# First attention of a two-layer block: the values' result turned ahead of the scores in two steps, and the last rows normalised a step sooner

## The reference

```
z    = einsum('nshd,ed->nshe', x, fm_w) + fm_b
v, k, q = (concat([exp(z), exp(-z)]) for x in (ctx, ctx, layernorm(x)))
scores  = einsum('nqhd,nkhd->nhqk', q, k) / sqrt(128)     # 16 heads of 16 features
attn    = softmax(scores)
out     = einsum('nhql,nlhd->nqhd', attn, v) @ fc_w.T + fc_b
x = x + out
```

## Time and profile before

| | |
|---|---|
| three runs | 350.15, 351.95 (median), 352.85 us |
| the profiled execution | 349.49 us, of which the span is 347.7 us |
| PE busy in the span | 303.8 us (87%) |
| DVE busy | 210.8 us (61%) |
| ACT busy | 166.4 us (48%) |
| POOL busy | 151.5 us (44%) |
| mean granted clock of TensorE | 0.973 of full speed |

### The profile page before, as it was taken

How to read it: one execution, slowest core, us unless ns; L and a number is a source line. 1 busy time by engine, 2 the same in 40 slices (tenths; PEclk the granted TensorE clock), 3 DMA queues, 4 the chain that set the end, 5 groups by cost and what they waited for, 6 DMA issues and landing times.

```text
span 347.7 us, 6257 instructions
## 1 busy us (share of the span) xinstructions
PE 303.8 (87%) x1956; PEld 208.6 (60%) x1957; DVE 210.8 (61%) x673; ACT 166.4 (48%) x276; POOL 151.5 (44%) x201
## 2 busy tenths in 40 slices
PE   7789799999988989899988977999999999999800
PEld 2344244545445547558865533788888888888700
DVE  5767375481558976857778696455455455455316
ACT  3567667667464545531555153444444444444314
POOL 5964796510102150110124056376666666664310
PEclk9999989999999999999999999999999999999965
DMA  7404130300000150000002100111111111122055
GB/s 210 142 2 160 58 154 1 126 0 6 0 1 2 38 205 1 3 0 2 0 0 74 49 0 27 28 56 47 47 45 46 45 45 45 45 45 38 25 163 214
DMA packets 9784, 19.08 MB, mean 55 GB/s; under 512 B 2337, under 2 KB 3713, under 8 KB 9761
## 3 DMA queue, kind: packets, MB, share of 16 engines
q1 hardware_dynamic: 7264, 13.67, 12.0%
q0 software_dynamic: 2496, 5.12, 5.5%
HBM read 13.99 MB, written 4.65 MB: 54 GB/s over the span
## 4 chain that ended last, share of the span: by engine, by line
PE 66%; DVE 18%; ACT 5%; DMA 4%; issue 3%; POOL 2%; SPq 1%; POOLq 0%; DVEq 0%; ACTq 0%
PE ps L1199 54%; PE ps L1705 5%; DVE xn L543 2%; DVE mx L588 2%; DMA dnT<-y_dram 2%; PE ps L1207 2%; PE ps L1304 2%; DVE stats L531 2%; PE ps L1680 1%; DVE hg L707 1%; ACT r_hot L1152 1%; PE ps L1311 1%; POOL rstd L366 1%; ACT dist L1147 1%; DVE g3r L631 1%
## 5 line engine op out<-in xcount | busy, mean ns | idle before, releaser
L490 POOL DMA_INDIRECT y_dram<-yb,dst_row x39 | 38.4, 986 | 32.2 <-DVE yb L932 31.9
L365 POOL TENSOR_SCALAR rstd<-mv 128x4 f32<-128x4 f32 x16 | 3.8, 236 | 99.7 <-DVE mv L534 99.7
L484 POOL DMA_INDIRECT xg<-xn_dram,src_row x39 | 38.0, 974 | 13.2 <-PE ps L1680 8.5
L1199 PE MATMUL ps<-dnT,hhT 128*128 x312 | 41.4, 275 | 0.6 <-DVE yb L932 0.6
L1167 ACT ACTIVATE gl<-ps 128x512 f32<-128x512 f32 x39 | 23.3, 597 | 38.6 <-PE ps L1199 38.6
L1199 PEld LDWEIGHTS ps<-dnT,hhT 128*128 128x128 f32 x312 | 37.8, 191 | 4.1 <-issue 0.8
L1046 ACT ACTIVATE ex<-ps 77x1024 f32<-77x1024 f32 x32 | 30.9, 1016 | 17.3 <-PE ps L1199 17.3
L588 DVE TENSOR_REDUCE mx<-ps 128x4 f32<-128x308 f32 x64 | 27.7, 472 | 18.9 <-PE ps L1199 18.2
L1173 ACT ACTIVATE hhT<-ps 128x512 f32<-128x512 f32 x39 | 23.3, 598 | 31.3 <-PE ps L1705 31.3
L1199 PE MATMUL ps<-uphi,xghi 128*128 x78 | 33.9, 435 | 1.1 <-DVE xglo L920 0.6
L918 DVE CAST xghi<-ps 128x128 fp32r<-128x128 f32 x39 | 11.4, 291 | 37.1 <-PE ps L1680 37.1
(11 more groups left out here) (229 smaller groups left out, 608.4 us busy)
## 6 DMA issues: line engine op xcount, KB each, us to landing
uplo<-in_up_dram SPq DMA_DIRECT2D x8, 512.0 KB, 4.4
dnT<-in_down_dram SPq DMA_DIRECT2D x8, 256.0 KB, 4.6
dnT<-y_dram SPq DMA_DIRECT2D x4, 512.0 KB, 6.3
xn_dram<-xn SPq DMA_DIRECT2D x4, 256.0 KB, 2.4
out_dram<-x SPq DMA_DIRECT2D x4, 256.0 KB, 2.4
x<-in_x_dram SPq DMA_DIRECT2D x3, 256.0 KB, 3.2
xg<-xn_dram,src_row POOLq DMA_INDIRECT x39, 2.7
y_dram<-yb,dst_row POOLq DMA_INDIRECT x39, 2.3
```

Source lines behind the costliest of these rows:

```text
L484: g.indirect_dma_start(xg[:, k % XR, :], None, xn_dram, bass.IndirectOffsetOnAxis(ap=src_row[:, k:k + 1], axis=0)).then_inc(gathered[k % X ...
L490: g.indirect_dma_start(y_dram, bass.IndirectOffsetOnAxis(ap=dst_row[:, k:k + 1], axis=0), yb[:, k % 2, :], None).then_inc(scattered[k % 2] ...
L1199: return pe.matmul(out_, lhsT, rhs, start=start, stop=stop, skip_group_check=True)
```

## The change

In steps 4 and 8, the first steps of batches 1 and 2, PE issues `turn_values(G - 2)` before `scores(G)` and no longer after it. In step 4 three products that nothing reads go ahead of it into bank 7, behind a wait for `normalise(1)`, which is the last reader of that bank. On DVE, the four instructions that normalise the rows of batch 3 move from the end of step 4 to the end of step 3, ahead of the two first maxima of step 4. Nothing is removed.

```diff
@@ VectorE, loop over G
-                if g == 0 and b + 2 < NB:
-                    layernorm_apply(0, b + 2)
+                if G in (0, NG - 1):
+                    layernorm_apply(0, 2 + G // (NG - 1))
@@ TensorE, loop over G
                 if G in (NG, 2 * NG):
                     for job in maxima(G, 0):
                         max_job(*job)
+                    if G == NG:
+                        pe.wait_ge(dve_on, G - 2)
+                        fill(3)
+                    turn_values(G - 2)
                 if turned:
                     queries(b + 2)
                 elif G < STEPS:
@@
-                if G >= 2:
+                if G >= 2 and G not in (NG, 2 * NG):
                     turn_values(G - 2)
                 if G >= 1:
                     values(G - 1)
```

## The result

The changed kernel took 346.71 us in the median of four runs (346.43 to 347.60), the kernel before 351.94 in four (350.15 to 352.85): ratio 0.986, 95% interval 0.982 to 0.991. Faster, by 5.2 us between these medians where the sum said 2.75. Twelve more runs of the changed kernel, alternating with the kernel before (experiment 7), give 0.990 (0.987 to 0.994), that is 3.4 us. Medians and ratios here leave out slow runs, those over 1.5% above the fastest of their kernel, such as two of twelve in each of experiments 1, 3, 4 and 9. The profiled execution took 346.59 us with a span of 344.8, against 349.49 and 347.7: 2.9 us.

A forecast was written before the change was run, and what follows sets the result against it. PE was taken to bound the kernel (66% of the chain), losing in step 4 to idling, half clock and late DVE. Terms -1.9 - 1.15 + 0.3 = -2.75 us gave a forecast median of 349.2, range 346.8 to 352.7.

The forecast's parts named there:

- the sum: Whole kernel: -1.9 in step 4, -1.15 in step 5, +0.3 in step 8, together -2.75 us.
- PE's queue and ACT: Steps 4 to 6: scores(5) near 45.0, released by ACT's exponentials, 0.2 behind PE's own queue; scores(6) at 49.0.
- The unread products hide: Step 4: three products (0.75) and the turn (0.53) fit the idle stretch at no cost, cutting it from 1.62 to 0.34.
- The moved xn instructions: Step 3 on DVE: POOL holds them from 37.93 to about 41.5, but maxima and normalise(2) stay in time, cost nothing.
- Step 8 costs 0.3: Step 8: the moved turn waits for ACT's copy and PE loses about 0.3, with bounds 0 and 0.85.
- The loss of step 4 is idle, half clock and late DVE in a row: Steps 4 and 5: three successive losses, with 1.9 us to gain in step 4 and 1.15 in step 5.
- the step that POOL's AFFINE_SELECTs don't hold DVE: Step 4 without half clock: xn instructions run unheld beside POOL's AFFINE_SELECTs, from about 45.7, done by 46.8.
- a rival with a chance of 0.20: Step 4: the clock doesn't fall in the timed runs, so the old order loses little; result 0, 352.0 us; chance 0.20.
- held all the same: Step 4: no clock fall, but POOL's AFFINE_SELECTs hold DVE's xn instructions until about 49.4; gain 2.1, 349.9 us; chance 0.07.
- a gain of more than 1%: Whole kernel: a measured time of 348.4 us or less, reached only with a lucky median; chance 0.20.
- its range: Whole kernel, measured time: 346.8 to 352.7 us, from the forecast's lower scatter to the no-clock-fall rival with its median's scatter.

The follow-up runs named there:

- experiment 7: Changed kernel run again with no edit, twelve runs alternating with the kernel before; median 348.22 us, ratio 0.990.
- experiments 1: Kernel before with only the four xn instructions of batch 3 moved to the end of step 3, PE's order as before; median 348.40 us, ratio 0.993.
- experiment 3: Changed kernel with step 8 put back as before, its turn no longer ahead of the scores; median 347.70 us, ratio 0.991.
- experiment 4: Changed kernel without the three unread products and their wait, both turns still ahead; median 349.58 us, ratio 0.995.
- experiment 9: Kernel before with only POOL reordered: b2 conversions first, selG and g3 built after the xn instructions; median 347.88 us, ratio 0.992.
- Experiments 5: Kernel before with only the three unread products and their wait added in step 4's idle stretch; median 352.05 us, ratio 1.001.
- experiment 6: Kernel before run and profiled again with no edit; median 351.17 us, ratio 1.000.
- Experiment 2: Changed kernel with the four xn instructions back at the end of step 4, PE's order kept; median 348.11 us, ratio 0.992.
- experiment 11: Kernel before with only seven more unread products in two later PE stalls; median 350.28 us, ratio 0.999.
- experiment 8: Changed kernel with seven more unread products in two later PE stalls; median 347.11 us, ratio 0.987.

## Why the prediction was right, and where its reasons were not

*PE's queue and ACT.* Right to 0.1: the sum had `scores(4)` to `scores(5)` at 3.2 and `scores(5)` to `scores(6)` at 4.0; measured 3.24 and 3.90, with ACT as the new releaser by 0.18, as said.

*The unread products hide.* Right: they and the turn take 1.09 of the idle 1.62, and 0.53 stay where the sum had 0.34.

*The moved xn instructions.* Right: DVE goes on to the maxima 3.43 us behind their start (38.10 to 41.53), where the sum had 3.5, and no one waits for it. (The fourth of them ends at 42.00, held by a MEMSET of POOL, but the maxima start beside it.)

*Step 8 costs 0.3.* Right: a wait of 0.30, and 0.33 by experiment 3.

*The loss of step 4 is idle, half clock and late DVE in a row.* The order of these was right, their shares were not. The prediction gave 1.9 us to step 4, for the turn in the idle stretch and the clock, and 1.15 to DVE's lateness. What failed is the step that POOL's AFFINE_SELECTs don't hold DVE, read from the earlier trace rows. From it followed that without the half clock the xn instructions would be done by 46.8 and the change be worth nothing, a rival with a chance of 0.20. Experiments 5 and 6 are that case, and in both the xn instructions end past 49.5 (49.54 and 49.62) and `scores(6)` come 12.9 behind `scores(3)`. The true split, at `scores(9)`: 0.63 for the clock of the one profiled execution (31.39 to 30.76) and 2.18 for the hold (30.76 to 28.58; experiment 9 takes away the hold alone and gets the same 28.58). The rival "held all the same", with a chance of 0.07, had the mechanism and 2.1 us; it is the one that the runs bear out, and it is a better account than the forecast's own.

*Its rule.* I said that the trace did not agree with the Trainium skill (SBUF — State Buffer, section "SBUF: two separate sides": GpSimd and VectorE in a two-port mode take a shared pair of ports exclusively for a whole instruction) for AFFINE_SELECT. Experiment 2 corrects that: the xn instructions end 0.08 to 0.09 behind the ends of a MEMSET and two AFFINE_SELECTs. So the trace agrees with the rule there, and not everywhere. In the earlier trace rows four xn instructions of 0.34 each ran beside this AFFINE_SELECT of 0.30 and four small MEMSETs, and none was held:

```profile
125.64 0.20 POOL L452 MEMSET lower<- 128x128 bf16 x1
126.27 0.20 POOL L452 MEMSET onesb<- 128x128 bf16 x1
126.54 0.10 POOL L452 MEMSET cnt<- 128x8 bf16 x1
126.70 0.22 POOL L452 MEMSET before<- 128x64 f32 x1
```

Nor does a long one hold them as such: at 188.80, in the same profile, four xn instructions took 1.12 while POOL ran a TENSOR_TENSOR of 128x4 f32 for 1.03 from 189.32. Those that held had 308 to 1232 elements in a row, those that did not 128 and fewer; only the IOTA of 128x128 in step 3 stands between (one xn instruction of 0.39 beside it in the changed kernel, ending 0.08 behind it). Why is not settled; the prediction's mistake was to carry what a small AFFINE_SELECT did in the earlier trace rows over to one of 24x512.

*The parts overlap.* DVE's move alone and PE's order alone each reach 28.6 at `scores(9)`, and so do both together. The move puts the hold where nobody waits for it; the order makes DVE early enough to be done just as POOL's first TENSOR_TENSOR of 1.15 starts (46.92 and 46.91 in experiment 2). At `scores(6)` PE's order gives 0.33 more than the move alone (10.39 against 10.72), and step 8 takes it back.

*The size.* The trace says 2.8 to 2.9, of which 0.6 is that the execution of before had a fall in step 4. The ratio of experiment 7 says 3.4 (2.0 to 4.7). The first 5.2 us of the medians of four were in part the luck of few runs. The prediction gave a chance of 0.20 to a gain of more than 1%, and the first four runs show 1.4%, experiment 7 just 1.0%. The median of 346.71 is even 0.1 below the lower end of its range, 346.8, while the 348.22 of experiment 7 lies within it.

What of the 3.4 goes beyond the 2.2 of the attention at full clock is not settled. Falls of the clock in step 4 explain little of it: each costs 0.6, of five profiled executions with this stall of 1.6 open (before, experiments 1, 6, 9 and 11) one had the fall, and filling the stall alone gave 1.001. The profiles of experiments 11 and 8 have no half clock before 328 us, in the kernel before and in the changed one; their spans are 347.8 and 344.7, and 2.14 of these 3.1 us lie between `scores(3)` and `scores(9)`. What the rest is, one execution of each doesn't tell.

## What to carry to other kernels

When a VectorE instruction lasts two to three times its usual time, look at GpSimd's row for the same time before looking at anything on the chain, and ask when that row ends: shifting the producer only helps if it moves the work past it. Two losses seen together in one profile are not two gains; a second profile of the same kernel, in which one of them happens to be missing, is a cheap experiment. And a turn or copy is worth pulling ahead only where the engine stands idle and the buffer is free: in step 4 both held and it brought 0.33 us, in step 8 neither did and it cost what its wait showed, 0.33.

## What was unexpected of the hardware

- Four fp32 TENSOR_SCALARs of 128x128 on VectorE take 1.11 us alone and 1.85, 2.79, 3.75 and 3.90 beside GpSimd. Between two instructions of GpSimd in a row, usually one of VectorE's gets through, so four of them can wait for four. MEMSETs and AFFINE_SELECTs of 24x512 hold them as TENSOR_TENSORs of that size do; MEMSETs and an AFFINE_SELECT of 128x128, and a TENSOR_TENSOR of 128x4 that runs for 1.03, don't. VectorE's maxima and `normalise`, which read PSUM, kept their 0.86 and 0.42 beside the same instructions.
- A PE stall of 1.62 ahead of `scores(4)` was followed by a granted clock of 0.50 in one execution of the kernel before and by 1.00 in another (1.63), as well as in experiments 1, 9 and 11. The same stall is no sure sign of a slower clock, and a profile with the half clock in it overstates what filling the stall brings: the fill alone brought nothing in twelve runs.
